# One-core graph layer: the edge products of a step in other bursts, the FFN's last products in one piece

## The reference

```python
agg = segment_sum(edge_weight[:, None] * xn[src], dst, num_segments=N)
gnn = relu(((1 + eps) * xn + agg) @ W1.T + b1) @ W2.T + b2
mix = ...            # hyperbolic maps, 256 -> 768 product, batch norm, 32-wide blocks, attention, 512 -> 256 product
x   = x + gnn + mix
x   = x + ffn(layernorm(x))   # 256 -> 1024 gelu -> 256 for the chosen half of the nodes, all others pass through
```

## Time and profile before

| | |
|---|---|
| median of 3 runs | 2568.11 us (2567.19 to 2571.41) |
| the profiled execution | 2566.61 us, its span 2564.2 us, mean granted TensorE clock 0.979 |
| busy: TensorE, its weight loads | 2398.2 us, 1789.8 us |
| busy: DVE, ACT, POOL | 1744.1, 1425.3, 1679.8 us |
| edge products on TensorE (L1355) | 4410 passes, 644.8 us busy |
| FFN products (L1450, L1462) | 1568 passes each, 369.7 and 359.5 us busy |
| chain that ended last | PE 49%, DVE 33%, ACT 10%, issue 4%, DMA 2% |

### The profile page before, as it was taken

One profiled execution on the slowest core, in us unless ns is written; L12 is line 12 of the kernel. 1 busy time (PEld: TensorE's weight loads), 2 busy tenths in 40 slices (PEclk: granted clock), 3 DMA queues, 4 the chain that ended last, 5 costly groups with the idle time before them and its releaser, 6 DMA issues.

```text
span 2564.2 us, 44369 instructions
## 1 busy us (share of the span) xinstructions
PE 2398.2 (94%) x13536; PEld 1789.8 (70%) x13536; DVE 1744.1 (68%) x5895; ACT 1425.3 (56%) x3219; POOL 1679.8 (66%) x1834
## 2 busy tenths in 40 slices
PE   4688999999999999999999999999999999999896
PEld 4675677776777776777777677777677777767686
DVE  7867667577675767757667676676766766767557
ACT  3546465565655655556556565565655656556431
POOL 1236777677776777777767777677777776777500
PEclk9789999999999999999999999999999999999998
DMA  6733444444444444444444444444444343444338
GB/s 209 245 114 97 132 117 120 116 114 130 119 122 115 114 122 118 127 120 113 122 114 115 132 119 121 113 115 125 116 127 119 113 126 110 117 128 118 90 119 286
DMA packets 225215, 327.42 MB, mean 128 GB/s; under 512 B 80845, under 2 KB 168510, under 8 KB 224956
## 3 DMA queue, kind: packets, MB, share of 16 engines
q0 software_dynamic: 84656, 231.94, 31.5%
q1 hardware_dynamic: 140300, 92.36, 12.4%
HBM read 285.70 MB, written 38.45 MB: 126 GB/s over the span
## 4 chain that ended last, share of the span: by engine, by line
PE 49%; DVE 33%; ACT 10%; issue 4%; DMA 2%; POOL 1%; SPq 0%; DVEq 0%
PE qkv L1450 14%; PE bank L1462 14%; PE bank L1355 8%; DVE rings L1154 5%; PE bank L1399 4%; PE qkv L1379 3%; ACT work L974 2%; DVE bank L1173 2%; DVE bank L1174 2%; DVE work L1179 2%; DVE bank L1167 2%; DVE bank L1178 2%; DVE work L1177 2%; PE bank L1369 2%; DVE work L1224 2%
## 5 line engine op out<-in xcount | busy, mean ns | idle before, releaser
L957 POOL DMA_INDIRECT rings<-xn_dram,window x1715 | 1652.1, 963 | 657.7 <-issue 403.9
L1355 PE MATMUL bank<-rings 128*64 128x256 f32 x4410 | 644.8, 392 | 12.8 <-DMA rings<-xn_dram,window 10.6
L1154 DVE TENSOR_SCALAR rings<-iota,window_dst,window 128x64 f32<-128x64 f32 (+1 forms) x1715 | 498.1, 343 | 215.2 <-PE bank L1355 204.2
L1355 PEld LDWEIGHTS bank<-rings 128*64 128x64 f32 x4410 | 309.5, 136 | 270.5 <-issue 117.1
L1450 PE MATMUL qkv<-work,ffn_weights 128*128 128x256 f32 x1568 | 369.7, 384 | 0.0
L1462 PE MATMUL bank<-ffn_weights,work 128*128 128x256 f32 x1568 | 359.5, 382 | 0.0
L1462 PEld LDWEIGHTS bank<-ffn_weights,work 128*128 128x128 f32 x1568 | 293.8, 190 | 54.0 <-issue 16.2
L1047 ACT ACTIVATE work<-qkv,fb 128x256 f32<-128x256 f32 x392 | 159.7, 472 | 305.4 <-PE qkv L1450 304.9
L1450 PEld LDWEIGHTS qkv<-work,ffn_weights 128*128 128x128 f32 x1568 | 292.2, 191 | 52.5 <-ACT work L1047 16.2
L1369 PE MATMUL bank<-resident,weights 128*128 128x256 f32 x1176 | 285.3, 386 | 0.0
L1369 PEld LDWEIGHTS bank<-resident,weights 128*128 128x128 f32 x1176 | 217.4, 191 | 44.4 <-ACT work L1060 15.4
(11 more groups left out here) (261 smaller groups left out, 3243.6 us busy)
## 6 DMA issues: line engine op xcount, KB each, us to landing
rings<-xn_dram,window POOLq DMA_INDIRECT x1715
xn_dram<-work SPq DMA_DIRECT2D x14, 896.0 KB, 8.6
work<-xn_dram SPq DMA_DIRECT2D x49, 256.0 KB
work<-in_x SPq DMA_DIRECT2D x48, 256.0 KB
out<-work SPq DMA_DIRECT2D x48, 256.0 KB
work<-in_x SPq DMA_DIRECT2D x7, 896.0 KB, 6.0
rings<-in_x SPq DMA_DIRECT2D x6, 896.0 KB, 11.5
rings<-out SPq DMA_DIRECT2D x6, 896.0 KB, 9.2
```

Of the source, the lines that this page charges most:

```text
L957: nc.gpsimd.indirect_dma_start(out=msg[G_ % RING][:, :], out_offset=None, in_=xn_dram[:, :], in_offset=bass.IndirectOffsetOnAxis(ap=window ...
L1154: v.tensor_scalar(one_hot(i, k, 0, len(quarters)), iota[:, quarters[0] * H:(quarters[-1] + 1) * H], window_dst[b][:, k:k + 1], window[b][: ...
L1355: te.matmul(agg[h][side * H:(side + 1) * H], one_hot(i, k, REACHES[k].index(q), 1), msg[gathered % RING], start=first, stop=n == STEP_PROD ...
```

## The change

It changes the tables, moves one call on ACT and two on TensorE.

- `PE_AT`: ft0 26 to 29, h2 30 to 33, ft1 38 to 39; `hid3` and `y2` are gone. Hidden 2 and 3 and the four projections follow each other, and `edges_to(STEP_PRODUCTS)` issues the products left over behind them, at the step's end.
- `DVE_AT`: the second `ft` from k = 36 to 32, `y` 4 to 5, `x` 3 to 7, the first `tail_out` 25 to 21, `stage` 22 to 21.
- ACT copies x3T before the sums.

```diff
-        PE_AT = dict(w1=2, w2=8, qkv=15, outT0=19, ft0=26, h2=30, outT1=34, ft1=38, hid3=41, y2=45)
-        DVE_AT = dict(scale=(6, 12), out=(8, 16), c=(15, 23), ft=(17, 36), sup=0, n4=1, f=7, y=4, x=3, combine=(9, 15), rstd=20, tail_out=(25, 30), stage=22)
+        PE_AT = dict(w1=2, w2=8, qkv=15, outT0=19, ft0=29, h2=33, outT1=34, ft1=39)
+        DVE_AT = dict(scale=(6, 12), out=(8, 16), c=(15, 23), ft=(17, 32), sup=0, n4=1, f=7, y=5, x=7, combine=(9, 15), rstd=20, tail_out=(21, 30), stage=21)
...
                     mix_n4_seed(j, tail)
+                    if m is not None:
+                        ffn_x3T(m)
                     tail_supT(j)
                     mix_exp(j)
                 mix_norms(i, 0)
                 mix_s_seed(i, 0, mix)
                 if j >= 0:
-                    if m is not None:
-                        ffn_x3T(m)
                     tail_g1(j)
...
                     ffn_hidden(m, 2, i)
-                edges_to(PE_AT["hid3"])
                 if m is not None:
                     ffn_hidden(m, 3, i)
...
                     ffn_project(m, 1, i)
-                edges_to(PE_AT["y2"])
                 if m is not None:
                     ffn_project(m, 2, i)
                     ffn_project(m, 3, i)
+                edges_to(STEP_PRODUCTS)
```

## The result

The changed kernel takes **2554.04 us** (median of 4 runs, 2553.42 to 2555.9) against 2568.24 of the kernel before on the same chip: a ratio of 0.9944, 95% interval 0.9927 to 0.9961. In a later comparison on one chip it took 2552.23 against 2568.44, 0.9934 (0.9920 to 0.9947). The profiled execution took 2555.9 us, its span is 2553.6 and the mean granted clock 0.981.

A forecast was written before the change was run, and what follows sets the result against it. TensorE, busy 94% of the span, and its few waits were taken to bound the kernel. Plain steps -24 us and steps after one without FFN +9 gave -15, from 2568.1 to 2553 us; range 2541 to 2566.

The forecast's parts named there:

- part 4: Plain steps: -0.6 us in 20 of the first kind, -0.77 in 15 of the second, -24 us in all.
- parts 1 to 3: Plain step: 10.49 us between the output turnings, 22.10 behind them, and x3T's copy off the seed-to-mix_v chain, 0.30 earlier.
- part 5: Step's sum on DVE (L1212), now after the step's last burst: in time for TensorE, with 1.5 us to spare.
- rival 4: DVE's sum (L1212) comes over 1.5 us late, so TensorE waits before L1407; 2581 us at 2.3 late; chance 0.05.
- part 6: FFN result, b2, first tail_out and second ft on DVE: moves fall into waits or slack and change nothing.
- part 7: SP and POOL queues: POOL waits at the 13th gather, later gathers come 0.5 to 0.65 us later; plain steps lose nothing.
- part 8: Step after one without FFN: burst of ten waits for the 23rd gather, +1.8 us in five steps, +9 us.
- rival 2: Slow clock after gather waits costs the five steps 2.6 us more each: 2566 us, no change; chance 0.12.
- part 9: Steps 0 to 2 and the last: gathers or DVE bind there, so 0, within 1 us.
- rival 1: Gathers don't bind in the burst of ten, so only the plain steps' gain counts: 2544 us; chance 0.13.
- rival 3: ACT's copy of x3T doesn't shorten the chain to the first turning: 2565 us, no change; chance 0.11.
- rival 5: The order has nine bursts, not eight, and 26 pairs for 25: products themselves gain nothing; no chance of its own.

The follow-up runs named there:

- Experiments 1 and 2: 1: kernel before with only ACT's x3T copy moved ahead of the sums' copy, 2552.81 us; 2: changed kernel with that copy put back, 2561.28 us.
- experiment 3: Changed kernel with its nine bursts cut so that no pair is parted (24 pairs, seven products behind the first turning): 2527.06 us, ratio 0.9849 to the kernel before.
- experiment 8: Changed kernel with DVE's work at its places of before, behind the new TensorE order: 2552.68 us, ratio 0.9949 to the kernel before.
- Experiment 7: Changed kernel with DVE's sum queued at product 6 in place of 0 and b2 at 4 in place of 7: 2581.48 us, ratio 1.0056 to the kernel before.
- bursts alone: Changed kernel with ACT's copy of x3T put back behind the seeds: 2561.28 us, ratio 0.9979 to the kernel before.
- the control: Changed kernel with 27 one-hot units in place of 30 and still 16 gather buffers: 2551.86 us, ratio 0.9938 to the kernel before.
- Experiment 5: Changed kernel with 17 gather buffers in place of 16, and 27 one-hot units in place of 30: 2545.87 us, ratio 0.9918 to the kernel before.
- the filled cut: Changed kernel with bursts recut to 24 pairs so that both turnings find DVE ready: 2513.02 us with 16 gather buffers, 2508.37 us with 17.
- the cut of seven: Changed kernel with bursts recut to 24 pairs, seven products behind the first turning: 2527.06 us with 16 gather buffers, 2514.16 us with 17.

## Why the prediction was right, and where it was not

**The sum of plain steps** (part 4) was -24 and is -24.1. The terms of parts 1 to 3 hold: 10.49 between the turnings (said: 10.49), 22.12 behind them (22.10), 1.00 from seed to mix_v (1.00). The first turning mostly comes 0.2 to 0.3 us earlier (said: 0.30 to 0.35). Experiments 1 and 2 show each half by itself; experiment 3 shows the price of a pair.

That the sum is met to 0.1 us is luck, as two errors cancel. Part 4 left the 15 steps of the second kind tied to DVE at the second turning. In the change no plain step waits there, the two kinds are gone, and these 15 gain 0.89 us each, not 0.77. The 20 of the first kind gain 0.54, not 0.62. That DVE is ready does not come from its new order, since with the order of before no plain step waits there either (experiment 8).

**Sum on DVE** (part 5): the sum starts 0.11 behind the burst and TensorE has 1.6 us to spare, where 1.5 was said. Experiment 7 drove it over that edge: rival 4 gave 2581 for a sum 2.3 us later, and 2.31 later made 2581.48. It is the mechanism by which this change could have lost, and DVE's waits in front of L1212 are what keeps it away. Timelines of TensorE (the group behind the burst) and of DVE in the change, at the end of step 19:

```profile
1095.22 0.33 PE L1378 MATMUL qkv<-ident,work 128*128 128x128 f32 x1
```

```profile
1094.47 0.35 DVE L1154 TENSOR_SCALAR rings<-iota,window_dst,window 128x128 f32<-128x128 f32 x1 [8.71 <-PE bank L1355]
1095.33 0.75 DVE L1212 SCALAR_TENSOR_TENSOR work<-work,cols,bank 128x512 f32<-128x512 f32 x1 [0.51 <-PE bank L1355]
```

**Other DVE moves** (part 6) cost and give nothing: experiment 8.

**Queues** (part 7): timeline of POOL, the 13th gather of step 17 and the 23rd of step 18 in the changed kernel, beside the earlier trace rows:

```profile
961.91 0.94 POOL L957 DMA_INDIRECT rings<-xn_dram,window  x1 [2.46 <-PE bank L1355]
...
1018.60 0.95 POOL L957 DMA_INDIRECT rings<-xn_dram,window  x1 [0.30 <-PE bank L1355]
```

POOL waits at the 13th, as said. The 23rd of step 18 stands 54.11 us behind the L1407 of step 17 (964.49), where it stood 53.49: +0.62, in the range of 0.5 to 0.65.

**The step behind a short one** (part 8) is the term that was mis-sized: +1.8 us each, +9, and it measured +14.4 in the first execution and +13.0 in the second. Two things are in that. With 2.4 GHz throughout (bursts alone) the five sum up to +10.2, and in the control, whose three short stretches at 1.2 GHz cost nothing that shows, to +9.7: 1.9 to 2.0 each, so the gathers' part was right. The other 3 to 5 us go with the slow clock of rival 2, which had 12 in 100 and came in part: a stretch of 6.8 us in three and in two of the five steps. The prediction left it out since most of it would fall into waits for gathers; that held for the stretches of 3.4 us and not for these. The Trainium skill, "TensorE: Matmul & The Clock Gate", section "HAM oscillation", tells of a kernel in which each group of products behind a wait for DMA starts on the slow clock; the trace agrees for the steps with a slow stretch and not for the others.

The *place* was wrong too. Part 8 let only the burst of ten wait, 2.9 us. Timeline of TensorE, changed kernel, step 18:

```profile
999.32 0.66 PE L1407 MATMUL bank<-ident,work 128*128 128x128 f32 x4 [0.51 <-DVE work L1212]
...
1006.00 1.11 PE L1355 MATMUL bank<-rings 128*64 128x256 f32 x6
1007.72 0.62 PE L1355 MATMUL bank<-rings 128*64 128x256 f32 x2 [0.60 <-DMA rings<-xn_dram,window]
...
1020.27 0.74 PE L1355 MATMUL bank<-rings 128*64 128x256 f32 x4 [0.58 <-DMA rings<-xn_dram,window]
1021.48 0.62 PE L1355 MATMUL bank<-rings 128*64 128x256 f32 x2 [0.46 <-DMA rings<-xn_dram,window]
```

L1407 waits 0.51 us for the sum, not 3.32, and the groups behind it run at 2.4 GHz, so that the burst of seven begins 6.7 us behind L1407 where it began 9.3. It gets there ahead of its gathers and takes 6.0 us in place of 2.0; the burst of ten loses another 1.8. The gathers' part came out right all the same (1.9 to 2.0 us for 1.8), since POOL sets it: from the 13th gather of the short step on it issues without a stop, 45 issues to the 23rd of the next, and where on the way TensorE waits for it makes no difference (experiment 8). Experiment 5 shows the size: one issue ahead, 1.21 us a pair.

**Steps 0 to 2 and the last** (part 9): steps 1 and 2 are 0.2 us longer. The last step's -2.6 goes with a stretch at 1.2 GHz, of 6.8 us in the kernel before, that this execution lacks; in the second one it is 3.4 us long and the difference -1.2. This was said as 0 within 1 us, and it is 0 within what executions differ by, which is more.

**The rivals.** Gathers do bind (rival 1 out, experiment 5), x3T was on the chain (rival 3 out, experiment 1), the sums come in time (rival 4, experiment 7), and rival 5 described the change well: 26 pairs for 25. The forecast of 2553 us lies between the two medians, and that is partly luck: in the profiled executions the differences are -10.6 and -13.1, not -15, as the pairs take 4.0 to 5.4 us more than was said and the last step gives back 1.2 to 2.6. The step on which the sign rested was part 4, and it was read from rows that measure each term directly.

## What to carry to other kernels

Where TensorE writes two half-tiles side by side, price an order by pairs, not by products or bursts: the same nine bursts, cut so that no pair is parted, gained 17 us more in the plain steps. Before moving work between engines, look at an idle engine's *order*: one copy that stood between two links of the chain cost 13.4 us in the plain steps, about as much as everything else in this change gained there. And where a queue has run ahead in long steps and is used up in short ones, follow it over both: here one buffer more was worth about one issue in each pair of steps (1.21 us against 1.25; 1.1 with the filled cut), and with the cut of seven 2.4, which is not all explained.

## What was not expected of the hardware

The granted clock of 0.50 (1.2 GHz) came in or behind bursts that wait for gathers, 0.5 to 2.1 us at a time, in one execution of a step and not in another of the same kernel. In the kernel before it began in or within 1 us behind the waits of 3.1 to 3.5 us for the sum, in all five steps behind a short one; in the change's first execution, with those waits down to 0.5 to 1.5 us, it stood in the bursts. What such a stretch costs goes by what follows it: a later wait for a gather takes it up, products that wait for nothing pass it on. The kernel with bursts alone had one such stretch between 300 and 2450 us of its span, of 3.4 us in step 48, and its mean clock of 0.986 is the highest of the profiled executions, though it is far from the fastest kernel.
